# Value sums of two neighbouring key tiles issued together in the three cross attentions of a four-layer decoder

## The chip, the cores and the metric

The kernel runs on one core of a Trainium2 chip. The core has TensorE (matmul, PE in the profile), VectorE (DVE), ScalarE (ACT), GpSimd (POOL) and SyncE (SP, which starts most DMAs). Each engine works through its own stream of instructions in order, and they wait for each other through semaphores. The metric is the device time of one execution in microseconds; lower is better.

## What is computed

A decoder of four layers on a batch of 4 sequences of 256 tokens, width 128. Each layer adds a self attention, a cross attention over 512 context tokens and a feed-forward part to the residual stream. The change is in the cross attentions of layers 0, 1 and 2. Layer 2's stands for all three; layer 0 adds a mask, layer 1 projections of queries, keys and values.

```
q, k, v = split(query), split(key), split(value)        # 16 heads of 8
scores = einsum('bhqd,bhkd->bhqk', q, k) / sqrt(8)
attn = softmax(scores, axis=-1)                         # over 512 keys
ctx = einsum('bhqk,bhkd->bhqd', attn, v)                # the value sums
x = x + merge(ctx) @ w_concat.T
```

Layer 3's cross attention has no softmax and is not touched.

## The kernel before

The three cross attentions are called X0, X1 and X2. Each does 4 batches x 16 heads. The unit of work is a step: two heads with a part of the queries or keys, 64 steps in each attention. The program of every engine is written by hand as a loop over slots, `cross_slot(use, t, ...)`, and every engine issues its share of slot `t` at the same place in the order. `LEAD` is 20: in slot `t` TensorE makes the scores of step `t` (for the row maxima) and the exponents' arguments of step `t - 20`. So slots 0 to 19 have scores alone, 20 to 63 both, 64 to 83 exponents alone, and slots 24 to 87 have sums.

In a slot TensorE does, in this order:

- `pair_step` (L632): the scores of two heads (L629) into one bank of a ring of two, `ps_s0` and `ps_s1`, and the exponents' arguments of two heads (L608) into the banks `ps_e0` and `ps_e1`, four of these in a slot, each bank filled in two halves. They alternate: e0, scores, e0, e1, scores, e1. In X0 a mask is put into each exponent bank first by a matmul with the identity (L606). A bank e0 or e1 is filled again only when ScalarE has taken the exponent of what was in it (`exped`), and a score bank only when VectorE has taken the maxima of it (`maxed`).
- after a batch's last scores, the turn of the maxima (L568).
- the value sums `sums(use, g, k, ...)` (L672), from 24 on: `g` is a group of four heads and `k` one of four key tiles of 128 keys. The four matmuls of one call (one for each head, f32, 32 columns each, side by side in the array) are shown by the profile as eight. All four `k` of a group add up in `ps_v`; after the last, ScalarE copies it (L1384, `lifted`) and only then may the next group start.
- the turn of the group copied last (L577, `turn_group`), every fourth slot, which takes a bank of the score ring too; VectorE normalises from it (L1895, L1903).
- at the end of a batch its close (L585), output projection (L593) and the turn for the next stage (L554).

ScalarE in a slot: the lift of a group where one is due, then the exponents of e0 and e1 (L1396). It writes them to a ring of seven buffers `pts`, and waits with `pt_free` until the sums of the step that lay there before are done. VectorE: the maxima of a score bank (L1860 in X0, L1864 in X1 and X2), and the rest.

The call with `k` needs the exponents of all four heads. The function `sums` waits for `exped` of the step `last_step`, here `4 * g + 2 + k // 2`: the same step for k=0 and k=1, and the next for k=2 and k=3. In slot `t` the call is that of `divmod(t - 24, 4)`.

X0's slots run behind the first self attention, with the start of the expert layer behind them. X1's first 20 are woven into the second self attention (`l1_attention`), its last behind the start of the next expert layer (`swiglu_tail`). X2's slots stand beside `l2_slot` and `chain`, the work on other batches of the layers before and behind.

Of the kernel before, what the change touches and what calls it, by code (L numbers as in the profile page):

```python
# [124 lines left out]
def close_slot(use, b):  # L125
    return 21 + 8 * b if use == A0 else 40 + 16 * b
# [116 lines left out]
def build(nc, d, out, ctx):  # L243
# [3 lines left out]
    def semaphore(name):  # L247
        return ctx.enter_context(nc.semaphore(name))
# [71 lines left out]
    def rows_by_head(tile):  # L320
# [66 lines left out]
    score_ps, maxed, exp_ps, exped, summed, lifted, turned, weighed = (  # L387
        semaphore(n) for n in ("score_ps", "maxed", "exp_ps", "exped", "summed", "lifted", "turned", "weighed"))
# [147 lines left out]
    def tensor_program():  # L536
# [3 lines left out]
        def claim(name):  # L540
            if name in free:
                pe.wait_ge(*free.pop(name))
# [21 lines left out]
        def turn_max(use, b, tile):  # L564
            n = BATCH0[use] + b + 1
            i = tile()
            pe.wait_ge(max_split, n)
            pe.transpose(ps_s[i][0:96, 0, 0:64].bitcast(BF16), mparts[:].rearrange("p a s c -> p (a s c)"),  # L568
                         ident_b[:]).then_inc(max_ps, 1)
            free[f"s{i}"] = (max_T, n)  # L570

        def turn_group(use, g, tile):
            n = GROUP0[use] + g + 1
            i = tile()
            pe.wait_ge(lifted, n)
            for q in range(TPB):
                m = pe.transpose(ps_s[i][:, 0, q * P:(q + 1) * P], outT[:, g % 2, q * P:(q + 1) * P], ident)  # L577
            m.then_inc(turned, 1)
            free[f"s{i}"] = (weighed, n)

        def turn_close(use, b):
            claim("m")
            pe.wait_ge(*closed_at(use, b))
            for i, t in enumerate(tiles(b)):
                m = pe.transpose(ps_m[:, i * P:(i + 1) * P], xn[:, t, :], ident)  # L585
            m.then_inc(close_ps, 1)
            free["m"] = (close_T, CLOSE_AT[use, b])

        def project_out(use, b, w, tile):
            i = tile()  # L590
            pe.wait_ge(close_T, CLOSE_AT[use, b])
            for j, t in enumerate(tiles(b)):
                m = pe.matmul(ps_s[i][:, 0, j * P:(j + 1) * P], qT[:, t * P:(t + 1) * P], w, start=True, stop=True)  # L593
            m.then_inc(out_ps, 1)
            free[f"s{i}"] = (x_done, X_AT[use, b])
# [68 lines left out]
        def sums(use, g, k, last_step, nkt, values):  # L664
            if k == 0:
                claim("v")
            pe.wait_ge(exped, 2 * (STEP0[use] + last_step) + 2)
            b = g // 4
            for j in range(GROUP):
                step = 2 * g + j // 2 if use == A0 else 4 * g + 2 * (j // 2) + k // 2  # L670
                pt = pts[use][step % len(pts[use])]
                m = pe.matmul(ps_v[j * COLS:(j + 1) * COLS, 0:S], values(b * nkt + k, g % 4 * GROUP + j),  # L672
                              pt[:, j % 2, k % 2, :], start=(k == 0), stop=(k == nkt - 1),
                              tile_position=(0, j * COLS))
            return m
# [125 lines left out]
        def cross_slot(use, t, w_out, following, tile=ring):  # L801
            if t == 0 and use != X0:
                pe.wait_ge(d_ones, 192)
                pe.wait_ge(d_cfill, CFILL[use])
            if t == LEAD[use] and use == X0:
                pe.wait_ge(farT_done, B)
            if t == LEAD[use] + 4:
                pe.wait_ge(d_vload, 16 * {X0: 1, X1: 2, X2: 3}[use])
            if t < STEPS[use] + LEAD[use]:
                pair_step(use, t, tile)  # L810
            if t % 16 == 1 and t > 1 and t < 80:
                turn_max(use, (t - 17) // 16, tile)
            g, k = divmod(t - LEAD[use] - 4, 4)
            if 0 <= g < 16:
                m = sums(use, g, k, 4 * g + 2 + k // 2, 4, cross_values)
                m.then_inc(summed, 1)
                free["v"] = (lifted, GROUP0[use] + g + 1)
            g, rest = divmod(t - LEAD[use] - 8, 4)
            if rest == 0 and 0 <= g < 16:
                turn_group(use, g, tile)  # L820
            for b in range(B):
                at = t - close_slot(use, b)
                if at == 2:
                    turn_close(use, b)
                if at == 3:
                    project_out(use, b, w_out, tile)
                if at == 6 and following:
                    turn_norm(following, b)
# [2292 lines left out]
```

## Time and profile before

| | us |
|---|---|
| median of 3 runs | 1241.89 |
| lowest, highest | 1233.96, 1242.09 |
| span of the profiled execution | 1242.7 |
| TensorE busy in it | 1039.3 (84%) |
| VectorE busy | 795.0 (64%) |
| ScalarE busy | 611.8 (49%) |
| chain that ended last: TensorE, VectorE, ScalarE | 62%, 27%, 5% |
| value sums of X0 to X2 (L672), matmuls busy | 132.4, 1536 of them |

The profiled execution is one run of the program under the hardware profiler; every duration below is from it, and its span is to be set beside the times of the runs without it.
### The profile page before, as it was taken

How to read it: one execution, taken by the hardware profiler on the slowest of the kernel's cores; microseconds unless marked ns; L12 is line 12 of the kernel's file. 1: busy time of each engine (PE TensorE's matmuls, PEld its weight loads, DVE VectorE, ACT ScalarE, POOL GpSimd, SP SyncE). 2: the span in 40 equal slices, each digit the busy share in tenths (PEclk: the TensorE clock that was granted, in tenths of full speed). 3: DMA queues.
4: the chain of work that ended last, by engine and by line, in shares of the span. 5: the costliest groups of instructions: out<-in, count | busy, mean ns of one | idle time of the engine just before them, and what ended most of it. 6: DMA issues, size and time to landing. Idle time of an engine off the chain costs nothing.

```text
span 1242.7 us, 19890 instructions
## 1 busy us (share of the span) xinstructions
PE 1039.3 (84%) x7649; PEld 556.7 (45%) x7649; DVE 795.0 (64%) x1984; ACT 611.8 (49%) x1018; POOL 252.3 (20%) x309
## 2 busy tenths in 40 slices
PE   5777699999899975788877889999658878869999
PEld 4233223333677652355542333566323334437757
DVE  7786867731315468887767883777687886575412
ACT  2456356666334437678753777323125555333342
POOL 2933400000000225577641000001131001000000
PEclk9789879999999986566765999999867888779999
DMA  8332140000000300077014202600102100000000
GB/s 303 95 89 69 39 167 2 2 2 1 1 1 1 102 35 1 1 216 143 1 45 141 101 2 36 109 1 3 49 26 72 59 1 2 34 1 1 1 9 9
DMA packets 34786, 61.25 MB, mean 49 GB/s; under 512 B 4771, under 2 KB 25076, under 8 KB 33092
## 3 DMA queue, kind: packets, MB, share of 16 engines
q1 hardware_dynamic: 33828, 58.64, 16.5%
q8 instruction: 62, 1.02, 0.3%
q10 hardware_dynamic: 864, 1.33, 0.3%
q14 instruction: 32, 0.26, 0.1%
HBM read 42.91 MB, written 16.65 MB: 48 GB/s over the span
## 4 chain that ended last, share of the span: by engine, by line
PE 62%; DVE 27%; ACT 5%; issue 4%; DMA 1%; POOL 1%; SPq 0%; DVEq 0%; ACTq 0%; POOLq 0%
PE ps_s L879 10%; PE ps_e L869 9%; PE ps_v L672 7%; DVE mx L1864 5%; PE ps_e L608 5%; PE ps_s L629 3%; PE ps_e L606 3%; PE ps_e L973 2%; DVE ps_s L1860 2%; DVE mx L1854 2%; PE ps_s L960 2%; ACT work L1396 2%; PE ps_s L1124 1%; PE ps_v L1144 1%; DVE work L2339 1%
## 5 line engine op out<-in xcount | busy, mean ns | idle before, releaser
L1396 ACT ACTIVATE work<-ps_e 128x512 f32<-128x512 f32 x448 | 250.7, 598 | 144.3 <-PE ps_e L608 139.1
L2618 POOL TENSOR_TENSOR rstd<-rstd,halves 128x2 f32<-128x2 f32 x52 | 36.6, 705 | 699.5 <-DVE rstd L1807 699.4
L1864 DVE TENSOR_REDUCE mx<-ps_s 128x2 f32<-128x1024 f32 x128 | 154.0, 1222 | 30.0 <-PE ps_s L629 28.5
L629 PE MATMUL ps_s<-ctx_stack,q_stack 49*128 49x512 bf16 (+1 forms) x384 | 129.0, 452 | 46.0 <-DVE mx L1864 33.7
L1498 ACT ACTIVATE work<-ps_s,keep 128x512 f32<-128x512 f32 x136 | 93.0, 687 | 140.3 <-PE ps_s L879 137.3
L608 PE MATMUL ps_e<-q_stack,ctx_stack 52*128 52x256 bf16 (+1 forms) x768 | 151.4, 298 | 9.1 <-ACT work L1396 3.6
L672 PE MATMUL ps_v<-work,vaug 128*32 128x256 f32 x1536 | 132.4, 421 | 4.6 <-ACT work L1384 4.6
L869 PEld LDWEIGHTS ps_e<-ffn_w,work 128*128 128x128 f32 x960 | 118.9, 197 | 21.6 <-issue 20.5
L879 PE MATMUL ps_s<-xnT,ffn_w 128*128 128x512 f32 x240 | 118.4, 617 | 3.6 <-ACT work L1498 3.6
L869 PE MATMUL ps_e<-ffn_w,work 128*128 128x128 f32 x960 | 120.7, 281 | 0.8 <-DVE x L2050 0.8
L2060 DVE SCALAR_TENSOR_TENSOR x<-ps_e,gates,x 128x128 f32<-128x128 f32 x128 | 38.9, 346 | 123.4 <-PE ps_e L869 120.3
L1860 DVE CUSTOM_DVE_ANT_0 ps_s<-ps_s,work 128x512 f32<-128x512 f32 x128 | 86.0, 717 | 29.1 <-PE ps_s L629 29.1
L608 PEld LDWEIGHTS ps_e<-q_stack,ctx_stack 52*128 52x128 bf16 (+1 forms) x768 | 45.0, 97 | 105.2 <-ACT work L1396 49.5
L629 PEld LDWEIGHTS ps_s<-ctx_stack,q_stack 49*128 49x128 bf16 (+1 forms) x384 | 29.6, 97 | 72.2 <-DVE mx L1864 46.7
L879 PEld LDWEIGHTS ps_s<-xnT,ffn_w 128*128 128x128 f32 x240 | 41.7, 195 | 41.9 <-issue 25.3
L672 PEld LDWEIGHTS ps_v<-work,vaug 128*32 128x32 f32 x1536 | 31.7, 112 | 49.8 <-issue 36.7
L606 PE MATMUL ps_e<-work,ident_b 128*128 128x512 bf16 x128 | 51.8, 404 | 2.3 <-issue 2.3
L2677 POOL TENSOR_TENSOR work<-work 128x1536 f32<-128x1536 f32 x14 | 47.9, 3441 | 0.9 <-ACT work L1642 0.8
L1376 ACT ACTIVATE xnT<-ps_m 128x256 f32<-128x256 f32 x36 | 13.7, 382 | 61.9 <-PE ps_m L554 60.1
L1854 DVE TENSOR_REDUCE mx<-ps_s 128x4 f32<-128x1024 f32 x32 | 38.1, 1220 | 9.4 <-PE ps_s L624 9.1
L1895 DVE RECIPROCAL rsum<-ps_s 128x8 f32<-128x8 f32 x48 | 9.7, 203 | 48.9 <-PE ps_s L577 48.7
L577 PE MATMUL ps_s<-keep,work 128*128 128x128 f32 x128 | 29.3, 312 | 12.9 <-ACT work L1384 6.5
(379 smaller groups left out, 1821.5 us busy)
## 6 DMA issues: line engine op xcount, KB each, us to landing
q_stack<-q_scr SPq DMA_DIRECT2D x32, 192.0 KB
ffn_w<-in_L0f_w SPq DMA_DIRECT2D x1, 4608.0 KB, 15.9
ffn_w<-in_L1f_w SPq DMA_DIRECT2D x1, 3456.0 KB, 12.9
q_scr<-parts SPq DMA_DIRECT2D x16, 192.0 KB, 2.1
c_scr<-ffn_w SPq DMA_DIRECT2D x12, 256.0 KB, 7.1
kx_scr<-ffn_w SPq DMA_DIRECT2D x12, 256.0 KB, 4.1
ctx_stack<-kx_scr SPq DMA_DIRECT2D x2, 1536.0 KB
ctx_stack<-c_scr SPq DMA_DIRECT2D x2, 1536.0 KB
```

What stands on the lines that cost most here:

```text
L606: pe.matmul(bank[name], ident_b[:], far_k[:, b, k:k + 2, :].rearrange("p k q -> p (k q)"), start=True, stop=False, skip_group_check=True)
L608: m = pe.matmul(bank[name][:, half * S:(half + 1) * S], stack[p0:p0 + n_rows, pair, k * P:(k + 1) * P], q_stack[p0:p0 + n_rows, b, pair, : ...
L629: return pe.matmul(ps_s[i][:, parity, :], q_stack[p0:p0 + n_rows, b, pair, part * P:(part + 1) * P], ctx_stack[p0:p0 + n_rows, pair, b * S ...
L672: m = pe.matmul(ps_v[j * COLS:(j + 1) * COLS, 0:S], values(b * nkt + k, g % 4 * GROUP + j), pt[:, j % 2, k % 2, :], start=(k == 0), stop=( ...
L869: m = pe.matmul(bank[name][:, i * P:(i + 1) * P], hid[:, j, (t0 + i) * P:(t0 + i + 1) * P], w2(e, j), start=(j == 0), stop=(j == FJ - 1))
L879: pe.matmul(bank[name], w1_of(st, e, j), xnT[:, g * 512:(g + 1) * 512], start=True, stop=True).then_inc(UPS[st], 1)
L1396: act.activation(pt[:, parity, :, :].rearrange("p k q -> p (k q)"), bank[f"e{parity}"], ACT.Exp).then_inc(exped, 1)
L1498: act.activation(hid_unit(st, u)[:, j, :], bank[f"h{n % 2}"], ACT.Gelu_apprx_tanh, bias=b1).then_inc(HIDS[st], 1)
L1854: m = dve.tensor_reduce(mx[:, b, :, pair, :], ps_s[i][:].rearrange("p a (q k) -> p a q k", q=TPB), AX, ALU.max, negate=True)
L1860: m = dve.tensor_tensor_reduce(ps_s[i][:, parity, :], ps_s[i][:, parity, :], far_q[:, b * TPB + part, :], 1.0, -3e38, ALU.add, ALU.max, mx ...
L1864: m = dve.tensor_reduce(mx[:, b, :, pair, part], ps_s[i][:], AX, ALU.max, negate=True)
L2677: pool.tensor_tensor(c, c, l1_s[:, HALVES[n], :], ALU.add).then_inc(added, 1)
```

## The change

The call of `sums` was made once in each of 64 slots. Now it is made in every second slot, where `k` is 0 or 2, for `k` and `k + 1` one after the other. The argument `last_step` is written as before with the even `k`; for `k + 1` it has the same value. The increments of `summed` are as many as before, and in the same order. ScalarE's, VectorE's, GpSimd's and SyncE's streams are the same, instruction for instruction.

```diff
--- before.py
+++ after.py
@@ -811,9 +811,9 @@
             if t % 16 == 1 and t > 1 and t < 80:
                 turn_max(use, (t - 17) // 16, tile)
             g, k = divmod(t - LEAD[use] - 4, 4)
-            if 0 <= g < 16:
-                m = sums(use, g, k, 4 * g + 2 + k // 2, 4, cross_values)
-                m.then_inc(summed, 1)
+            if 0 <= g < 16 and k % 2 == 0:
+                sums(use, g, k, 4 * g + 2 + k // 2, 4, cross_values).then_inc(summed, 1)
+                sums(use, g, k + 1, 4 * g + 2 + k // 2, 4, cross_values).then_inc(summed, 1)
                 free["v"] = (lifted, GROUP0[use] + g + 1)
             g, rest = divmod(t - LEAD[use] - 8, 4)
             if rest == 0 and 0 <= g < 16:
```

Two places in TensorE's stream. The first is in X0, where scores are made: from the second half of the exponents of slot k=0 (`ps_e1`) over the sums (`ps_v`) and the group's turn (L577) to the first score matmul of the next slot. Before:

```order
L608 MATMUL ps_e1<-q_stack,ctx_stack 128x256
L629 MATMUL ps_s1<-ctx_stack,q_stack 128x512
L608 MATMUL ps_e1<-q_stack,ctx_stack 128x256
L672 MATMUL ps_v<-work,vaug 32x256 x4
L577 MATMUL ps_s0<-keep,work 128x128 x2
L606 MATMUL ps_e0<-work,ident_b 128x512
L608 MATMUL ps_e0<-q_stack,ctx_stack 128x256
L629 MATMUL ps_s1<-ctx_stack,q_stack 128x512
```

And with the change:

```order
L608 MATMUL ps_e1<-q_stack,ctx_stack 128x256
L629 MATMUL ps_s1<-ctx_stack,q_stack 128x512
L608 MATMUL ps_e1<-q_stack,ctx_stack 128x256
L672 MATMUL ps_v<-work,vaug 32x256 x8
L577 MATMUL ps_s0<-keep,work 128x128 x2
L606 MATMUL ps_e0<-work,ident_b 128x512
L608 MATMUL ps_e0<-q_stack,ctx_stack 128x256
L629 MATMUL ps_s1<-ctx_stack,q_stack 128x512
```

The sums of k=1, which stood behind the next slot, now stand ahead of the turn; the score bank that the last row waits for is the one that slot k=0 filled. The second place is in X1, where only exponents are left: from one group's turn on. Before:

```order
L577 MATMUL ps_s1<-keep,work 128x128 x2
L608 MATMUL ps_e0<-q_stack,ctx_stack 128x256 x2
L608 MATMUL ps_e1<-q_stack,ctx_stack 128x256 x2
L672 MATMUL ps_v<-work,vaug 32x256 x4
L608 MATMUL ps_e0<-q_stack,ctx_stack 128x256 x2
L608 MATMUL ps_e1<-q_stack,ctx_stack 128x256 x2
L672 MATMUL ps_v<-work,vaug 32x256 x4
L554 MATMUL ps_m<-keep,xn 128x128 x2
L608 MATMUL ps_e0<-q_stack,ctx_stack 128x256 x2
L608 MATMUL ps_e1<-q_stack,ctx_stack 128x256 x2
L672 MATMUL ps_v<-work,vaug 32x256 x4
```

And with the change:

```order
L577 MATMUL ps_s1<-keep,work 128x128 x2
L608 MATMUL ps_e0<-q_stack,ctx_stack 128x256 x2
L608 MATMUL ps_e1<-q_stack,ctx_stack 128x256 x2
L608 MATMUL ps_e0<-q_stack,ctx_stack 128x256 x2
L608 MATMUL ps_e1<-q_stack,ctx_stack 128x256 x2
L672 MATMUL ps_v<-work,vaug 32x256 x8
L554 MATMUL ps_m<-keep,xn 128x128 x2
L608 MATMUL ps_e0<-q_stack,ctx_stack 128x256 x2
L608 MATMUL ps_e1<-q_stack,ctx_stack 128x256 x2
```

The exponents' matmuls of slots k=1 and k=2 (e0, e1, e0, e1) now follow each other with nothing between, and the sums of both key tiles come after; it is the same with slots k=3 and k=0 further down, where the batch's last slots have L554 or L593 between them.

## Rows read from the trace of the kernel before

**Rows 1.** The page: span, and one costly group (busy us, mean ns).
```profile
span 1242.7 us, 19890 instructions
...
PEclk9789879999999986566765999999867888779999
...
L1864 DVE TENSOR_REDUCE mx<-ps_s 128x2 f32<-128x1024 f32 x128 | 154.0, 1222 | 30.0 <-PE ps_s L629 28.5
```

**Rows 2.** Busy time by stretch (length, PE, PEld, DVE, ACT, POOL, clock, DMA).
```profile
720.00:770.00 50.00, 46.64 (x476) 17.11 (x472) 29.07 (x75) 39.67 (x81) 1.39 (x2) 1.00 0.01 2
...
960.00:1000.00 40.00, 32.34 (x256) 11.89 (x257) 34.17 (x61) 20.34 (x42) 0.70 (x1) 0.82 0.19 75
```

**Rows 3.** Timeline, TensorE, X0 (start, us, engine, line, operation, count, idle before).
```profile
200.94 0.39 PE L606 MATMUL ps_e<-work,ident_b 128*128 128x512 bf16 x1
...
202.23 0.64 PE L672 MATMUL ps_v<-work,vaug 128*32 128x256 f32 x8
202.80 0.44 PE L577 MATMUL ps_s<-keep,work 128*128 128x128 f32 x2
203.07 0.38 PE L606 MATMUL ps_e<-work,ident_b 128*128 128x512 bf16 x1
203.39 0.28 PE L608 MATMUL ps_e<-q_stack,ctx_stack 56*128 56x256 bf16 x1
203.80 0.39 PE L629 MATMUL ps_s<-ctx_stack,q_stack 49*128 49x512 bf16 x1
```

**Rows 4.** Timeline, ScalarE, the same slot of X0.
```profile
201.70 1.27 ACT L1396 ACTIVATE work<-ps_e 128x512 f32<-128x512 f32 x2 [0.24 <-PE ps_e L608]
```

**Rows 5.** Timeline, VectorE, end of that slot's maxima.
```profile
203.60 0.14 DVE L1860 DVE_READ_ACCUMULATOR2_ANT mx<- 128x1 f32 x1
```

**Rows 6.** Timeline, TensorE, X2, slots before the first sums.
```profile
924.55 0.28 PE L608 MATMUL ps_e<-q_stack,ctx_stack 52*128 52x256 bf16 x1
...
925.64 0.28 PE L608 MATMUL ps_e<-q_stack,ctx_stack 52*128 52x256 bf16 x1 [0.48 <-ACT work L1396]
```

**Rows 7.** Timeline, TensorE, end of X0, two sums in a row.
```profile
295.39 1.07 PE L672 MATMUL ps_v<-work,vaug 128*32 128x256 f32 x16
296.39 1.12 PE L879 MATMUL ps_s<-xnT,ffn_w 128*128 128x512 f32 x2
```

**Rows 8.** Timeline, TensorE, X1, slots without scores.
```profile
750.92 0.88 PE L608 MATMUL ps_e<-q_stack,ctx_stack 52*128 52x256 bf16 x4
751.73 0.64 PE L672 MATMUL ps_v<-work,vaug 128*32 128x256 f32 x8
...
753.38 0.88 PE L608 MATMUL ps_e<-q_stack,ctx_stack 52*128 52x256 bf16 x4
```

**Rows 9.** Timeline, TensorE, X1, a clean group with scores.
```profile
723.95 0.44 PE L577 MATMUL ps_s<-keep,work 128*128 128x128 f32 x2
724.32 0.28 PE L608 MATMUL ps_e<-q_stack,ctx_stack 52*128 52x256 bf16 x1
724.77 0.39 PE L629 MATMUL ps_s<-ctx_stack,q_stack 49*128 49x512 bf16 x1 [0.17 <-DVE mx L1864]
...
729.70 0.44 PE L577 MATMUL ps_s<-keep,work 128*128 128x128 f32 x2
```

**Rows 10.** Timeline, TensorE, X1, first exponents of a batch.
```profile
696.18 0.28 PE L608 MATMUL ps_e<-q_stack,ctx_stack 52*128 52x256 bf16 x1 [0.79 <-DMA q_stack<-mT]
```

**Rows 11.** Timeline, TensorE, X2, a stall and a filler.
```profile
996.68 0.60 PE L629 MATMUL ps_s<-ctx_stack,q_stack 49*128 49x512 bf16 x1 [2.53 <-DVE mx L1864]
...
1006.88 1.60 PE L1279 MATMUL ps_s<-ffn_w,work 128*128 128x128 f32 x12
```

**Rows 12.** Timeline, TensorE, X1 at half clock, without and with sums.
```profile
671.09 0.39 PE L608 MATMUL ps_e<-q_stack,ctx_stack 52*128 52x256 bf16 x1 [0.27 <-ACT work L1396]
...
672.39 0.39 PE L608 MATMUL ps_e<-q_stack,ctx_stack 52*128 52x256 bf16 x1 [0.21 <-ACT work L1396]
...
677.12 0.39 PE L608 MATMUL ps_e<-q_stack,ctx_stack 52*128 52x256 bf16 x1
...
679.11 0.39 PE L608 MATMUL ps_e<-q_stack,ctx_stack 52*128 52x256 bf16 x1
```

## The prediction

> **What bounds the kernel now.** I read the page first: one core, span 1242.7 us [rows 1]. The three cross attentions lie at about 160 to 300 us (X0), 650 to 775 us (X1) and 900 to 1080 us (X2). Then the busy time by stretches [rows 2]: in the middle of X1 TensorE is busy 46.64 of 50 us at full clock, in X2 32.34 of 40 us at a mean clock of 0.82. So X1 is close to TensorE-bound by its busy time and X2 is not. What limits a step, though, is read from the timeline, and there the three differ. I call one pass of `cross_slot` a slot, and by what follows from `k` the four slots of a head group P0 (k=0, with the turn of the finished group behind its sums), P1, P2, P3.
>
> In X0 a slot has two mask matmuls more, so TensorE is the limit: from 200.94 to 202.80 is one slot of 1.86 us, 1.29 of it the exponents' and scores' matmuls and 0.57 the sums (202.23 to 202.80) [rows 3]. ScalarE starts on the exponents 0.76 us after the slot begins and takes 1.27 us for both banks [rows 4], with slack. Only in P1 is there a stall: it begins at 203.07, its first score matmul would come 0.33 us later but comes at 203.80, 0.40 us late, because the ring of two score banks waits for VectorE, which is done with P0's scores at 203.74 [rows 3, 5].
>
> In X1 and X2 the same matmuls without the mask take only about 0.54 us, and 0.57 us of sums stand between two of them. What sets the pace there is the loop bank e0, exponent on ScalarE, bank free again. The rows that show this best are two slots of X2 before its sums have begun, with nothing between them: they begin at 924.55 and 925.64, 1.09 us apart, the second after 0.48 us of waiting for the exponent [rows 6]. So without sums between them two slots are no closer than 1.09 us, and with sums between them they are 1.11 us (0.54 + 0.57) apart. **The sums now fill a gap in which TensorE would wait anyway.** This decides the forecast.
>
> **What the change does.** No instruction is added or taken away: 3 x 16 groups x 4 sums, each 4 matmuls that the profile counts as 8. The sums of k=1 and k=3 come one slot earlier, behind those of k=0 and k=2. Their waits on `exped` name the same step as their neighbour's, so no new wait arises. The last sum of a group is there a slot earlier, but ScalarE lifts it at its old place. P1 and P3 lose their sums; P0 and P2 have two; P0's two now stand ahead of the turn.
>
> *Fewer changes of form.* Eight sum matmuls take 0.57 us until the next operation starts. Sixteen in a row take 1.00 us (295.39 to 296.39) [rows 7]. So a pair costs 1.00 us in place of 1.14: 0.14 us saved, 96 pairs, 13.4 us if TensorE were the limit everywhere. The Trainium skill ("TensorEngine Tiling", Key Properties) says that changing the tiling mode drains TensorE; the row agrees, with 0.14 us for a change and its way back, and by that rule alone the kernel would be the 13.4 us faster.
>
> *X0.* Slot pairs P1-P2 and P3-P0 now follow directly. The second one's first matmul needs bank e0, free after 0.76 us and half of 1.27 us and some hand-over, at 1.40 to 1.42 us; the slot is 1.29 us long. That is 0.11 to 0.13 us of new wait against 0.14 saved: zero. In P1 the 0.40 us stall goes, since the second sum now lies ahead of it (0.43 us, 1.00 less 0.57) and VectorE is done by then. Scores are still made in 9 such P1 slots behind a turn: 9 x 0.42 = **-3.8 us**.
>
> *X1, slots without scores* (the last five groups). Now a pair lasts from 750.92 to 753.38, 2.46 us; a slot whose bank e1 has to wait for its exponent lasts 0.81 us up to its sums (750.92 to 751.73) [rows 8]. Afterwards a pair is 1.09 to the second slot, 0.81 for it, 1.00 for the double sums: 2.90 us. That is +0.44 a pair, two pairs a group: 5 x 0.87 = 4.4. At the close of a batch four projection matmuls fall between P3 and P0 and cover the wait once: -0.4. **+4.0 us.**
>
> *X1, slots with scores* (ten groups). A clean group lasts 5.75 us from turn to turn (723.95 to 729.70), with a stall of 0.45 us in P1 (724.32 to 724.77) on VectorE's maxima [rows 9], which take 1.22 us each [rows 1]. Afterwards: 0.37 (turn) + 1.09 + 0.81 + 1.00 + 1.09 + 0.81 + 1.00 = 6.17 us: +0.42. VectorE needs 4 x 1.22 and under half a microsecond for the turn, 5.3 us, so it is no longer what is late; ScalarE's loop is. In other words both second halves cost 0.43, and P1's stall takes one of them back. Where the next batch's maxima come by DMA (a wait of 0.79 us ahead of the slot at 696.18) [rows 10], the other is taken in too; that is so twice. 10 x 0.42 - 2 x 0.4 = 3.4, and 0.2 less for the start at half clock (below). **+3.2 us.**
>
> *X2.* The same per clean group, but other work stands between its slots. The stall at 996.68, 2.53 us on VectorE, swallows a shifted sum whole, and twelve matmuls of 1.60 us at 1006.88, between P1 and P2, keep the exponent's wait covered, so that there the 0.14 is earned [rows 11]. Of the 16 groups I find five or six clean or nearly so (+0.42 each), the others at zero, a few below. Bounds: nothing at all, and 16 x 0.6 = +9.6. I take **+2 us**, near the lower end, since most of its stalls name VectorE.
>
> *Half clock.* Part of X1 and X2 runs at 1.2 GHz. There a slot is 1.99 us (677.12 to 679.11) and two slots without sums are 1.30 us apart (671.09 to 672.39) [rows 12]. A pair then takes 1.30 + 0.98 + 1.02 + at most 1.02 = 4.3 us against 3.98: +0.3 at most, less than at full clock.
>
> Sum: -3.8 + 4.0 + 3.2 + 2 = **+5.4 us**, 1248.1 on the profiled execution's 1242.7. That execution lies 0.8 us above the median of the runs shown (1241.9), so I predict **1247 us**.
>
> **Rivals.**
> *A, TensorE-bound after all (faster).* If ScalarE's loop took up the burst, 13.4 us of form changes and the 3.8 us of X0 would come off: 1225 us. For it speaks the busy share in X1 [rows 2]. Against it speak the two slots 1.09 us apart: TensorE waits in them with nothing else to do [rows 6]. It would decide if two bare slots took less than 1.46 us together (2.46 - 1.00), where the rows make it 1.90. A tenth of the chance; a smaller form of it, X0 gaining and X2 gaining from its covered pairs, ends within 1%.
> *B, all absorbed (same).* The loss in X1 is swallowed by VectorE and DMA waits as in X2, the gain in X0 stays: 1238 to 1242. For it: the stalls in [rows 9 to 11]. Against it: the five groups without scores have no such stall to give [rows 8].
> *C, the clock (slower).* TensorE idles about 0.5 us in each pair of X1 where it idled little. In X2 the clock, down to 0.82 in the mean, goes with TensorE's idle stretches [rows 2, 11]. If X1 fell to half clock for half its 32 pairs, each of these would take 4.3 in place of 2.9 us: 16 x 1.4 = 22 us, 1269 in all. A third of that is 1255. Against it: the bare slots at 924.55 are half idle and still run at full clock. The Trainium skill ("TensorE: Matmul & The Clock Gate", Part 1) has it that the throttled state is the default and that activity releases it; no run here shows yet how the new rhythm is judged.
>
> **How the numbers follow.** Forecast mechanism as sized (1243 to 1253) 0.58; B 0.17; C, or a loss in X2 near its upper bound, 0.16; A 0.09. One per cent, 12.4 us, is about what a measurement of this kernel can tell from no change. Above 1254.3 lie C but for its mildest cases and the tail of the forecast: 0.19. Below 1229.5 lies A: 0.08. The range 1237 to 1259 takes in B and the first third of C, and leaves out A and the rest of C, under 2 in 10.
>
> **What the profile afterwards would show.** In X0 no score matmul waits 0.4 us behind the turn, and the slot pairs last 3.7 us. In X1 slots without scores come in pairs of 2.9 us, with TensorE's idle time named after the exponents. ScalarE's idle time falls between double sums, about 0.7 us at a time. The groups with scores last 6.2 us and VectorE's stall in P1 is gone. X1 from its first sum to its last is 7 us longer, X0 4 us shorter. Wrong I would be if X1's pairs took less than 2.6 us (A), if the groups with scores kept 5.75 us (B), or if the granted clock in X1 fell below 1 (C).

## The result, and the profile after

| | before | after |
|---|---|---|
| median, lowest, highest (us) | 1241.99 (1233.96 to 1246.52) | 1265.7 (1263.25 to 1269.77) |
| ratio | | 1.0195, 95% interval 1.0156 to 1.0233 |
| span of the profiled execution | 1242.7 | 1265.0 |
| mean granted clock in it | 0.863 | 0.850 |

The kernel became 23.7 us slower. I had said 1247 us and a range up to 1259, so the forecast was wrong in size and right in sign. The page of after, to be set beside [rows 1]:

```profile
span 1265.0 us, 19890 instructions
...
PEclk9778879999999985567676997999756889779999
...
L1864 DVE TENSOR_REDUCE mx<-ps_s 128x2 f32<-128x1024 f32 x128 | 154.4, 1222 | 33.6 <-PE ps_s L629 30.5
```

The maxima take 1222 ns as before. In the clock line the 25th place (about 760 to 790 us, in X1) fell from 9 to 7, and the 29th to 31st, around X2's start, from 8, 6, 7 to 7, 5, 6. The busy time by stretches, for [rows 2]:

```profile
720.00:770.00 50.00, 40.31 (x392) 16.55 (x388) 31.83 (x74) 32.17 (x66) 0.70 (x1) 0.90 0.01 2
960.00:1000.00 40.00, 32.74 (x276) 13.14 (x276) 29.56 (x56) 21.71 (x44) 3.53 (x6) 0.79 0.28 100
```

In the middle of X1 TensorE is busy 40.31 us of 50 instead of 46.64, ScalarE 32.17 instead of 39.67, and the clock is 0.90 where it was 1.00.

A clean group of X1 with scores, TensorE's timeline (start, us, engine, line, operation, count, idle before), for [rows 9]:

```profile
730.88 0.44 PE L577 MATMUL ps_s<-keep,work 128*128 128x128 f32 x2
731.25 0.28 PE L608 MATMUL ps_e<-q_stack,ctx_stack 52*128 52x256 bf16 x1
...
732.35 0.28 PE L608 MATMUL ps_e<-q_stack,ctx_stack 52*128 52x256 bf16 x1 [0.48 <-ACT work L1396]
...
733.16 1.07 PE L672 MATMUL ps_v<-work,vaug 128*32 128x256 f32 x16
...
737.06 0.44 PE L577 MATMUL ps_s<-keep,work 128*128 128x128 f32 x2
```

From turn to turn it takes 6.18 us (730.88 to 737.06); the forecast was 6.17. Two slots without sums are 1.10 us apart with 0.48 us of waiting for the exponent, and the double sums take 1.01 us (733.16 to the next slot at 734.17). ScalarE's idle time lies between double sums, as its timeline of the same group shows:

```profile
731.70 2.20 ACT L1396 ACTIVATE work<-ps_e 128x512 f32<-128x512 f32 x4 [0.84 <-PE ps_e L608]
734.60 1.08 ACT L1396 ACTIVATE work<-ps_e 128x512 f32<-128x512 f32 x2 [0.70 <-PE ps_e L608]
```

The part of X1 without scores, for [rows 8]: one pair at half clock, one at full clock.

```profile
763.22 0.61 PE L608 MATMUL ps_e<-q_stack,ctx_stack 52*128 52x256 bf16 x4
764.51 1.09 PE L608 MATMUL ps_e<-q_stack,ctx_stack 52*128 52x256 bf16 x4 [0.68 <-ACT work L1396]
765.53 1.93 PE L672 MATMUL ps_v<-work,vaug 128*32 128x256 f32 x16
767.39 0.69 PE L577 MATMUL ps_s<-keep,work 128*128 128x128 f32 x2
...
774.74 0.40 PE L608 MATMUL ps_e<-q_stack,ctx_stack 52*128 52x256 bf16 x4
775.82 0.88 PE L608 MATMUL ps_e<-q_stack,ctx_stack 52*128 52x256 bf16 x4 [0.68 <-ACT work L1396]
776.63 1.07 PE L672 MATMUL ps_v<-work,vaug 128*32 128x256 f32 x16
777.63 0.44 PE L554 MATMUL ps_m<-keep,xn 128*128 128x128 f32 x2
```

At full clock a pair lasts 2.89 us (774.74 to 777.63; forecast 2.90, before 2.46). At half clock it lasts 4.17 us (763.22 to 767.39). So the groups of X1 are what I worked out; but part of them runs at half clock, where in the trace of before all of this part ran at full clock.

**The measure used below.** A run's granted clock is a mean over two levels, 1.2 and 2.4 GHz, so the time at half clock is 2 x (1 - clock) x span. From the two pairs, a microsecond at half clock costs (4.17 - 2.89) / 4.17 = 0.31 us. With that the difference of two kernels is split in two: what the clock accounts for, and the rest. The split is an estimate: it takes the price of one place for the whole program. The runs bear it out roughly: among the runs of before, the span grows with the time at half clock by 0.26, 0.29 and 0.30 us per us in three series and by 0.18 in the fourth. At 0.27 the clock's shares below would be an eighth smaller.

### The profile page after: what moved, and what is told of

The parts are those of the page before. It is cut to its first block, busy times and chain, and to the rows that moved or that the text cites. A ratio compares the mean times of both kernels' runs of the same rounds, so it can differ in the third digit from the quotient of the medians.

```text
span 1265.0 us, 19890 instructions
## 1 busy us (share of the span) xinstructions
PE 1041.4 (82%) x7649; PEld 571.3 (45%) x7649; DVE 795.8 (63%) x1984; ACT 608.8 (48%) x1018; POOL 252.1 (20%) x309
## 4 chain that ended last, share of the span: by engine, by line
PE 62%; DVE 25%; ACT 6%; issue 4%; DMA 1%; POOL 1%; SPq 0%; DVEq 0%; ACTq 0%; POOLq 0%
PE ps_s L879 10%; PE ps_e L869 9%; PE ps_v L672 8%; PE ps_e L608 5%; DVE mx L1864 5%; ACT work L1396 3%; PE ps_s L629 3%; PE ps_e L606 3%; PE ps_e L973 2%; PE ps_s L960 2%; DVE mx L1854 2%; DVE ps_s L1860 1%; PE ps_s L577 1%; PE ps_s L1124 1%; PE ps_v L1144 1%
## 5 line engine op out<-in xcount | busy, mean ns | idle before, releaser
L1396 ACT ACTIVATE work<-ps_e 128x512 f32<-128x512 f32 x448 | 251.2, 599 | 161.1 <-PE ps_e L608 155.5
L1864 DVE TENSOR_REDUCE mx<-ps_s 128x2 f32<-128x1024 f32 x128 | 154.4, 1222 | 33.6 <-PE ps_s L629 30.5
L672 PE MATMUL ps_v<-work,vaug 128*32 128x256 f32 x1536 | 117.7, 430 | 5.6 <-ACT work L1384 5.6
L672 PEld LDWEIGHTS ps_v<-work,vaug 128*32 128x32 f32 x1536 | 43.3, 118 | 50.9 <-issue 21.9
L577 PE MATMUL ps_s<-keep,work 128*128 128x128 f32 x128 | 30.9, 327 | 12.1 <-ACT work L1384 6.6
```

What stands on the lines that cost most here:

```text
L1396: act.activation(pt[:, parity, :, :].rearrange("p k q -> p (k q)"), bank[f"e{parity}"], ACT.Exp).then_inc(exped, 1)
L1864: m = dve.tensor_reduce(mx[:, b, :, pair, part], ps_s[i][:], AX, ALU.max, negate=True)
```

## The experiments

Line numbers behind line 815 are shifted by a few lines in some of these kernels, so the sums' exponents are L1396 in one and L1400 or L1405 in another.

### The change as a whole, and each attention alone

The whole change again, and X0, X1 and X2 changed alone, each with this condition (X1's is shown):

```diff
             g, k = divmod(t - LEAD[use] - 4, 4)
+            if 0 <= g < 16 and use in (X1,):
+                if k % 2 == 0:
+                    for kk in (k, k + 1):
+                        sums(use, g, kk, 4 * g + 2 + k // 2, 4, cross_values).then_inc(summed, 1)
+                    free["v"] = (lifted, GROUP0[use] + g + 1)
-            if 0 <= g < 16:
+            elif 0 <= g < 16:
                 m = sums(use, g, k, 4 * g + 2 + k // 2, 4, cross_values)
```

> The changed kernel once more, for a second trace and more times. Theory L (the exponent loop: the sums covered ScalarE's exponent, and where nothing covers it TensorE waits): the groups of X1 without scores last 6.2 us, those with scores 6.2, whatever the clock does elsewhere; X1 from its first sums to its last is 7 us longer than before at full clock. Theory K (the clock: most of the 23 us come from stretches at half clock that the idle gaps bring about): the half clock stretches lie again in X1's last third and in X2, and the time follows their number. If the 4.6 us that the first profile was behind before any changed slot is chance, they are not there this time.

> Only X0 issues its sums in pairs. My prediction's step: 9 stalls of 0.4 us go, the pairs cost nothing: -3.8 us. The profile of the changed kernel showed X0 level instead (VectorE's last slots of X0 as late as its first). Theory L: between -4 and +1 us. Theory K: the same, with any loss in a half clock stretch inside X0.

> Only X1 issues its sums in pairs. Theory L: +7 us, of it 4 in the five groups without scores and 3 in the ten with scores, 6.2 us a group; up to +9 with the end of X1. Theory K: +12 or more, of it 4 or more in a half clock stretch in the part without scores, as in the first profile of the change. No effect of X1: within 2 us.

> Only X2 issues its sums in pairs. Theory L: +2 us, since VectorE's stalls and other work cover it (bounds 0 to +10). Theory K: +5 to +10 with more half clock stretches in X2 and behind it, where the layers after X2 were 3 us later in the first profile of the change. The parts should add up to the whole within 3 us under L; under K they need not.

Measured beside 23 runs of before with a median of 1241.83 us. The span column is the difference of the mean spans; "half clock" is the mean time at half clock over all runs of the kernel, less that of before (333 us) in the same series; "rest" is the span column less 0.31 times the half clock. All but the ratio are in us.

| kernel | median, ratio (interval) | span | half clock | x 0.31 | rest |
|---|---|---|---|---|---|
| whole change | 1264.1, 1.0167 (1.0129 to 1.0204) | +21.5 | +35 | 10.8 | 10.7 |
| X0 alone | 1242.95, 1.0008 (0.9983 to 1.0033) | +1.0 | +4 | 1.4 | -0.4 |
| X1 alone | 1256.1, 1.0098 (1.006 to 1.0136) | +13.6 | +15 | 4.8 | 8.7 |
| X2 alone | 1248.39, 1.0038 (1.0016 to 1.006) | +5.5 | +8 | 2.5 | 3.0 |

The medians add up: 1.1 + 14.3 + 6.6 = 22.0 us, beside 22.3 for the whole. X0 gives nothing, X1 costs twice its forecast and X2 three times. About half of the loss goes with the clock. The standard error of the mean time at half clock is 2 to 6 us for each kernel, so each split is good to 1 to 2 us only.

The 4.6 us that the first profile of the change lay behind ahead of any changed slot were chance: X0's first sums stand at 168.83 us in before, 173.43 in after, 168.67 in the whole change again, and at 172.36 in x1_tail below, which leaves X0 alone.

**X0.** Where the gain of 3.8 us went is seen in single groups of X0. TensorE's timeline of before, the group in which the turn of the maxima (L568) stands in P1:

```profile
185.36 0.44 PE L577 MATMUL ps_s<-keep,work 128*128 128x128 f32 x2
...
188.07 0.64 PE L672 MATMUL ps_v<-work,vaug 128*32 128x256 f32 x8
...
189.45 0.39 PE L629 MATMUL ps_s<-ctx_stack,q_stack 49*128 49x512 bf16 x1 [0.21 <-DVE mx L1860]
...
190.41 0.64 PE L672 MATMUL ps_v<-work,vaug 128*32 128x256 f32 x8
```

And with X0 alone changed:

```profile
179.08 0.44 PE L577 MATMUL ps_s<-keep,work 128*128 128x128 f32 x2
...
186.79 0.44 PE L577 MATMUL ps_s<-keep,work 128*128 128x128 f32 x2
...
190.87 0.39 PE L629 MATMUL ps_s<-ctx_stack,q_stack 49*128 49x512 bf16 x1 [0.85 <-DVE mx L1865]
...
191.83 1.07 PE L672 MATMUL ps_v<-work,vaug 128*32 128x256 f32 x16
...
196.60 0.44 PE L577 MATMUL ps_s<-keep,work 128*128 128x128 f32 x2
...
211.42 0.39 PE L629 MATMUL ps_s<-ctx_stack,q_stack 49*128 49x512 bf16 x1 [0.43 <-DVE mx L1865]
```

The group ahead (179.08 to 186.79) takes 7.71 us instead of 8.10: its stall is gone, as forecast. In the group with L568, P2's score matmul comes 4.08 us after the turn, before it was 4.09: VectorE, which has to take the turned maxima out of the score bank, sets that moment. The sums of P1 used to run inside this wait; now the wait is 0.85 us instead of 0.21, and the double sums stand behind it. The group takes 9.81 us instead of 9.33. P1's own stall stays as well in this group (0.69 us before, 0.68 now). So the gain of 0.39 in one group is given back in the next.

From turn to turn the nine groups with scores behind a turn (g = 1 to 9) come in three kinds. The five odd ones gain 0.38 to 0.40 each, 2.0 us together. The two that close a batch (g = 4 and 8) gain nothing, 9.06 and 9.07 us for 9.04: P1's stall is gone, but behind the output projection (L593), which takes a score bank too, stands a new one of 0.43 us, at 211.42. Of those with L568, g = 2 loses 0.48, and g = 6 takes 11.30 us for 9.34. The busy time of that last group, before and with X0 alone changed:

```profile
220.26:229.60 9.34, 8.44 (x71) 2.73 (x68) 6.55 (x21) 5.14 (x10) 0.00 (x0) 1.00 0.02 4
```

```profile
221.40:232.70 11.30, 9.62 (x72) 3.15 (x68) 6.97 (x23) 5.00 (x9) 0.00 (x0) 0.85 0.02 4
```

Its clock is 0.85, and its double sums take 1.87 us (226.79 to 228.66) instead of 1.00: about 3 us at half clock, some 1.5 us of time. Each of the four traces with all of X0 in pairs (after, the whole change again, this one, fill below) has one group of 11.30 to 11.32 us among its two with L568 inside X0's scores (g = 2, 6), the other being 9.81 or 9.82; the two traces of before have 9.33 and 9.34 us there. So even in X0, which I had held to be the safe gain, the clock has a share.

### Only the end of X1 (x1_tail)

```diff
-            if 0 <= g < 16 and use in (X1,):
+            if 0 <= g < 16 and use == X1 and g >= 10:
```

> Pairs only in the last six groups of X1, which have no scores beside them (24 slots). By the forecast's terms +4.0 us and nothing else. If X1's further loss of some 6 us is the clock and arises where TensorE idles at each pair without any scores to fill, it is here: +10 us, with a stretch at half clock in the trace. If it arises in the groups with scores, +4 us and full clock.

Measured 1250.45 us, ratio 1.0067 (1.0035 to 1.0098); mean span +7.8 us. This part can be cut out exactly in every trace: from the router's matmul (L836, `ps_m<-keep,xnT 128x8`) to the first matmul of the next feed-forward part (L960, 128x512). The busy time by stretches between these two, for before, this kernel, X1 alone, and the whole change again:

```profile
745.96:773.09 27.13, 25.29 (x267) 9.51 (x263) 8.38 (x42) 21.67 (x44) 0.69 (x1) 1.00 0.15 25
```

```profile
744.87:782.10 37.23, 30.58 (x258) 11.57 (x254) 8.38 (x42) 21.64 (x43) 0.70 (x1) 0.72 0.11 18
```

```profile
747.97:785.21 37.24, 30.58 (x258) 11.60 (x254) 8.38 (x42) 21.64 (x43) 0.69 (x1) 0.73 0.10 16
```

```profile
751.59:788.11 36.52, 29.77 (x259) 11.44 (x255) 8.39 (x42) 21.63 (x43) 0.70 (x1) 0.77 0.20 29
```

The columns are length, busy time of TensorE (and of its weight loads), VectorE, ScalarE and GpSimd, granted clock, DMA share and GB/s. The first trace of after has 35.33 us at 0.81. Take off 0.31 us for each us at half clock (20.8, 20.1, 16.8 and 13.4 us): 30.8, 31.0, 31.3 and 31.2 us are left, against 27.13. **That is +3.7 to +4.2 us, and the forecast's term for this part was +4.0.** The other 4 to 6 us are the clock. Half-clock time of 13 to 21 us stands in this part in all four traces, where the first trace of before had none. Over the 12 runs of x1_tail the picture is weaker: their time at half clock is 5 us above that of before, with a standard error of 7 (single runs lie between 293 and 377 us), which makes 1.5 us by the clock and 6.3 rest. So the 20.8 us in its trace are not what each of its executions shows.

### Before, once more (same)

> The kernel before once more, for a second trace of it: which of its stretches at half clock lie at the same place again, and how far the lengths of X0, X1 and X2 agree between two executions of one program. If the stretches at half clock are set by the program, X1 has none in its last 50 us here too; if chance has a part in them, it may have one of 3 to 10 us, as the kernel with X0 alone changed had.

Its span was 1242.9 us, and in the same stretch:

```profile
743.56:773.55 29.99, 28.65 (x267) 9.97 (x263) 8.38 (x42) 21.84 (x44) 0.70 (x1) 0.83 0.12 22
```

So chance has a part: the same program lost 2.9 us there to 10.2 us at half clock (0.28 us each). With X0 alone changed the stretch is 29.95 us at 0.83, with X2 alone 28.16 at 0.94; the three kernels warm, x0_some and both further down, which leave this part alone, have 27.14 us at 1.00 each. So seven traces without the pairs have 1.00 (four of them), 0.94, 0.83 and 0.83, and the four with them 0.72, 0.73, 0.77 and 0.81. The two groups do not overlap, but the change makes more of something that was there already.

### Filling the gaps (fill)

The changed kernel with sum matmuls that nobody reads, in the slots with k=1 of X1 and X2, where TensorE waits for ScalarE:

```diff
+            if 0 <= g < 16 and k == 1 and use != X0 and t < STEPS[use] + LEAD[use]:
+                for j in range(GROUP):
+                    pe.matmul(ps_v[j * COLS:(j + 1) * COLS, S:2 * S], vaug_pad[:, 0:COLS], keep[:, 0:S],
+                              start=False, stop=True, tile_position=(0, j * COLS), skip_group_check=True)
```

> The changed kernel with four more sum matmuls (0.57 us at full clock) in each slot with k=1 of X1 and X2, where TensorE now waits for ScalarE; they write the second half of ps_v, which nobody reads, 32 times in all. Theory L (ScalarE sets the pace: two slots without sums are 1.09 us apart, and 0.54 + 0.57 fits in it): they cost at most 1 us where the clock stays, so about 1264 us again, and the slot pairs of X1 keep 2.9 us. Theory K (part of the loss is the clock, which falls because TensorE idles in the gaps): X1 stays at full clock and the time falls towards 1256 us. Rival, TensorE is the bound: 32 x 0.57 = 18 us more, 1282 us.

Measured 1258.41 us, ratio 1.0148 (1.0113 to 1.0183). 32 times 0.57 us = 18 us of matmuls were added, and the kernel took 5.7 us less than without them by the medians, and 4.5 by the mean spans, with a standard error of 1.9. The same stretch of X1:

```profile
749.65:786.12 36.47, 32.09 (x290) 11.92 (x286) 8.39 (x42) 21.48 (x43) 0.70 (x1) 0.77 0.20 30
```

It is as long, and at the same clock, as in the whole change again (36.52 us at 0.77), with 2.3 us more of TensorE's time in it. The rival "TensorE is the bound" (1282 us) falls: what is put into the gaps is free. Over the six runs the time at half clock was 11 us above that of before, not 35: 3.5 us by the clock, 13.5 rest. Theory K gets its direction, but not in full: X1's end did not return to full clock.

### The pair in the other slots (late)

```diff
             if 0 <= g < 16:
-                m = sums(use, g, k, 4 * g + 2 + k // 2, 4, cross_values)
-                m.then_inc(summed, 1)
-                free["v"] = (lifted, GROUP0[use] + g + 1)
+                if k % 2:
+                    for kk in (k - 1, k):
+                        sums(use, g, kk, 4 * g + 2 + k // 2, 4, cross_values).then_inc(summed, 1)
+                    free["v"] = (lifted, GROUP0[use] + g + 1)
```

> The pairs in the other slots: P1 has the sums of k=0 and k=1, P3 those of k=2 and k=3, in all three attentions. The turn of the finished group now stands alone between P0 and P1. Theory L: in X1 and X2 the turn (0.37 us) lies in a gap in which TensorE waits for ScalarE, so a clean group of X1 takes 5.80 us instead of 6.17 (before: 5.75), and a group costs about 0.4 us less than in the changed kernel: 16 in X1 and the clean ones of X2, some 8 to 9 us. In X0 nothing is gained, since VectorE's maxima hold up P1 just as before and the longer sums come behind them: 9 x 0.43 = 3.9 us more than before. Sum about 1264 - 9 + 3 = 1258 us. If the loss had nothing to do with the place of the pair but only with its length, 1264 us again. Theory K adds: X1 at full clock again, 1252.

Measured 1249.2 us, ratio 1.0075 (1.0043 to 1.0106), 15 us less than the change with as many pairs of the same length. TensorE's timeline in the part of X1 without scores:

```profile
756.64 1.07 PE L672 MATMUL ps_v<-work,vaug 128*32 128x256 f32 x16
757.64 0.40 PE L608 MATMUL ps_e<-q_stack,ctx_stack 52*128 52x256 bf16 x4
758.72 0.88 PE L608 MATMUL ps_e<-q_stack,ctx_stack 52*128 52x256 bf16 x4 [0.68 <-ACT work L1397]
759.53 1.07 PE L672 MATMUL ps_v<-work,vaug 128*32 128x256 f32 x16
760.53 0.40 PE L608 MATMUL ps_e<-q_stack,ctx_stack 52*128 52x256 bf16 x4
761.20 0.41 PE L577 MATMUL ps_s<-keep,work 128*128 128x128 f32 x2 [0.27 <-ACT work L1385]
761.61 0.87 PE L608 MATMUL ps_e<-q_stack,ctx_stack 52*128 52x256 bf16 x4
762.42 1.07 PE L672 MATMUL ps_v<-work,vaug 128*32 128x256 f32 x16
```

A group lasts 5.78 us (756.64 to 762.42; expected 5.80): the turn at 761.20 now lies in the gap between two slots without sums. The stretch to the feed-forward part takes 29.18 us, wholly at full clock:

```profile
752.19:781.37 29.18, 24.66 (x272) 10.53 (x271) 8.38 (x42) 22.89 (x45) 0.70 (x1) 1.00 0.17 28
```

2.05 us more than before, with half of the gaps covered. The expected 1258 us without the clock, 1252 with it, were still too high; the runs spent 328 us at half clock, 6 less than before. The rest, +11.0 us, hardly differs from that of the change (10.7), because X1 gains what X0 loses: from first turn to last, X0 takes 125.44 us in late and 122.66 in after (before: 123.03), and X1, with 0.31 us taken off for each us at half clock, 96.3 against 98.5. By this measure the clock makes nearly all of the difference between the two kernels.

### A sum inside the slot (mid)

One sum a slot, as before, but in X1 and X2 those of k = 1, 2 and 3 between the matmuls for bank e0 and those for e1 (the place in `pair_step` only; `cross_slot` passes the sum in as `between`):

```diff
             if exps:
                 exps_of(use, h, 0, 1)
+                if between:
+                    between()
                 exps_of(use, h, 1, 0)
```

> The other way round: one sum a slot as before, but in X1 and X2 the sums of k=1, 2 and 3 stand inside their slot, between the second half of bank e0 and the first of e1, so that ScalarE has an exponent to take while they run. Theory L: ScalarE's gaps behind the sums (0.3 us a slot pair in the part of X1 without scores) close; a pair there goes from 2.46 to 2.24 us, 2 us in all, and where VectorE is late nothing changes: 1232 to 1240 us. Rival: VectorE's maxima and the order of the banks bound it, 1242 us. If the scores behind the sums now come too late for VectorE, it is slower: 1250.

Measured 1278.4 us, ratio 1.0271 (1.0219 to 1.0323): slower than everything else here, where I expected a gain. Two rows of ScalarE's timeline in X1 at full clock give the part of it that is order:

```profile
731.87 2.28 ACT L1405 ACTIVATE work<-ps_e 128x512 f32<-128x512 f32 x4 [0.32 <-PE ps_e L608]
734.46 0.60 ACT L1405 ACTIVATE work<-ps_e 128x512 f32<-128x512 f32 x1 [0.32 <-PE ps_e L608]
```

The exponent of e0 takes 0.60 us, and in that time TensorE does 0.57 us of sums and only then 0.27 us for e1, so ScalarE runs dry. A group takes 6.31 us (turns at 729.70 and 736.01). More than half of the loss is the clock: 405 us at half clock, 71 more than before, 22 of 37 us by the price above; without its two longest runs (1285.76 and 1288.31 us) it is 56 more, 17 of 33 us. In X1's end:

```profile
765.00:780.00 15.00, 15.00 (x91) 4.43 (x92) 2.70 (x12) 8.04 (x16) 0.70 (x1) 0.50 0.00 1
780.00:795.00 15.00, 13.36 (x84) 3.53 (x88) 0.86 (x4) 8.48 (x16) 0.00 (x0) 0.50 0.22 37
```

TensorE is busy 15.00 of 15.00 us by its records and has half its clock, and it keeps that clock through the next 15 us, 13.36 of them busy. So "TensorE idles, and therefore the clock falls" is too simple. The Trainium skill ("TensorE: Matmul & The Clock Gate", Part 1) says that throttling is the default and activity releases it; this row does not agree, as far as activity is what the records call busy.

### A version that beats both

Two small edits of the kernel before. First, the unread sums in the four slots of X1 and of X2 that have no sums yet, [rows 6]:

```diff
+            if use != X0 and LEAD[use] <= t < LEAD[use] + 4:
+                for j in range(GROUP):
+                    pe.matmul(ps_v[j * COLS:(j + 1) * COLS, S:2 * S], keep[:, 0:COLS], keep[:, 0:S],
+                              start=False, stop=True, tile_position=(0, j * COLS), skip_group_check=True)
```

> The kernel before, with four more sum matmuls into the unread half of ps_v in each of the four slots of X1 and of X2 that have no sums yet (t = 20 to 23), where TensorE waits 0.48 us for ScalarE: eight times 0.57 us. Theory L (a gap filled with work costs nothing): 1242 us. Theory K (the clock falls where TensorE waits, and rises again where it does not): the stretch at half clock at X1's start, which reaches about 20 us beyond the start of these slots in the kernel before, ends earlier, and the time falls by up to 0.3 us for each us less at half clock, 1236 to 1240 us. Rival, TensorE-bound: 8 x 0.57 = 4.6 us more, 1246 us.

Second, in X0 the pair k=0, k=1 in those groups alone where nothing gives the gain back:

```diff
             if 0 <= g < 16:
-                m = sums(use, g, k, 4 * g + 2 + k // 2, 4, cross_values)
-                m.then_inc(summed, 1)
+                early = use == X0 and g < 10 and g % 2 == 1
+                for kk in ((0, 1) if k == 0 else () if k == 1 else (k,)) if early else (k,):
+                    sums(use, g, kk, 4 * g + 2 + k // 2, 4, cross_values).then_inc(summed, 1)
```

> X0 alone is changed, and only k=0 and k=1 of the groups g = 1, 3, 5, 7 and 9 are issued together: those in which no turn of maxima (L568) follows in P1. X1 and X2 as before. Theory from the trace of x0_only: these groups lose the stall of P1 and take 7.71 us instead of 8.11 from turn to turn, 5 x 0.4 = 2 us off, and the groups with a turn of maxima keep their 9.33 us: 1240 us. Rival, the stall only moves to P3, where the next group's sums now stand as before: 1242 us.

And both together:

> The kernel before with the two small changes that each came out a little below it: four unread sum matmuls in each of the slots t = 20 to 23 of X1 and X2, and in X0 k=0 and k=1 issued together in the groups g = 1, 3, 5, 7 and 9. If both gains are real they add up: 2 us from X0's stalls and 2 to 6 us from less time at half clock in X2, 1233 to 1237 us. If warm's was chance: 1239 us.

Measured beside before's 1240.66 us (23 runs; the first two) and 1240.69 us (17 runs; both):

| kernel | median | ratio (interval) | span | half clock |
|---|---|---|---|---|
| fillers in slots 20 to 23 (warm) | 1239.04 | 0.9976 (0.9952 to 1.0) | -2.9 | -16 |
| X0's clean groups paired (x0_some) | 1238.27 | 0.9995 (0.9966 to 1.0023) | -1.0 | 0 |
| both | 1232.94 | 0.9951 (0.9926 to 0.9975) | -6.8 | -21 |

The two together are the one kernel here whose interval lies clearly below 1: 0.5% under before. The mean spans have standard errors of 1.3 to 1.6 us, so that 6.8 is more than 2.9 and 1.0 together proves nothing; nearly all of the 6.8 us goes with the clock (21 us at 0.31). Its profiled execution is the shortest with the highest clock, from the view of spans and clocks:

```profile
core 0: 1225.8 us, clock 0.884
```

Of warm, TensorE's timeline at the start of X2, beside [rows 6]:

```profile
924.99 0.28 PE L608 MATMUL ps_e<-q_stack,ctx_stack 52*128 52x256 bf16 x1
...
925.53 0.64 PE L816 MATMUL ps_v<-keep 128*32 128x256 f32 x8
926.10 0.28 PE L608 MATMUL ps_e<-q_stack,ctx_stack 52*128 52x256 bf16 x1
```

The slots are 1.11 us apart with the filler and were 1.09 apart without it: the gap takes it in. The busy time of the stretch behind it, first before, then warm:

```profile
924.00:960.00 36.00, 29.61 (x231) 10.47 (x229) 28.29 (x43) 19.57 (x39) 7.16 (x7) 0.76 0.13 39
```

```profile
924.00:960.00 36.00, 29.70 (x288) 10.94 (x286) 31.62 (x47) 22.69 (x45) 7.17 (x7) 0.95 0.20 61
```

The clock is 0.95 instead of 0.76. With both edits it is 0.95 too, and in the second trace of before 0.76 again. Three further traces without fillers in which X2's first sums come within 3 us of warm's (x0_some, x2_only, x0_only) have 0.76, 0.78 and 0.79. Over 150 us from X2's first value sum on, the clock is 0.82 and 0.83 in the two traces of before and 0.83 to 0.86 in eight of the other kernels without fillers (mid: 0.75), 0.89 in warm, and 0.91 in both and in fill. The other engines get further in the same 36 us. At X1's start, where I had expected it, nothing moved. In the trace of x0_some a pair of groups takes 17.03 us instead of 17.43:

```profile
178.99 0.44 PE L577 MATMUL ps_s<-keep,work 128*128 128x128 f32 x2
...
186.26 0.44 PE L577 MATMUL ps_s<-keep,work 128*128 128x128 f32 x2
...
196.02 0.44 PE L577 MATMUL ps_s<-keep,work 128*128 128x128 f32 x2
```

I had expected 7.71 and 9.33; it is 7.27 and 9.76, since the turn in the odd groups itself stands 0.43 us later, behind two sums. The sum is the expected one: 0.40 us for each of five groups, 2 us. X0 from its first sum to its last turn shows it: 129.43 us in x0_some and in both, 131.46 and 131.47 in the two traces of before. The comparison of whole times alone can't tell it from nothing.

## Why the prediction was wrong

**What held.** The reading of what paces X1: two slots without sums stay 1.08 to 1.10 us apart, the double sums take 1.0 us, pairs last 2.89 us and groups 6.18 us, where I had 2.90 and 6.17. VectorE's stall in P1 is gone there. X1's end costs 3.7 to 4.2 us at equal clock, where I had 4.0. Rival A is excluded: 18 us of further matmuls cost nothing, and rival B too: the groups did not keep 5.75 us. One thing in my words was too narrow: I named the loop of bank e0. At 1.08 to 1.10 us for two banks (the rows at 734.60 and 731.70 in after's ScalarE timeline) ScalarE itself takes as long as the loop, so with nothing between the slots it is simply full. For the sum it makes no difference.

**The step that failed first: the clock.** The sum put the clock's change at nothing and left it to rival C, which had a chance of 0.16 (with a large loss in X2) and whose price was X1's alone (22 us if half its pairs fell, 1255 for a third of that). The runs have 35 to 44 us more at half clock in the whole program: 11 to 14 us. C's sign came: the granted clock in X1 fell below 1; but it did so in the second trace of before too (0.83 in X1's end), so that sign alone could not tell the change from chance. In the traces X1's end, with 13 to 21 us at half clock, gives 4 to 6 us, and X0 some 1.5. Behind X2's last turn, where no instruction is changed, five of the traces with pairs in X1 or X2 (after, the whole change again, X1 alone, X2 alone, fill) take 164.0 to 164.1 us at a clock of 0.91, and four others (the two of before, X0 alone, x1_tail) 160.9 at 0.93: 3 us more, which the forecast had nowhere. The remaining five (late, mid, warm, x0_some and both) take 159.4 to 162.4 us. The remaining part can't be placed: from X2's first value sum on, 150 us have a clock of 0.83 in after and 0.85 in the whole change again, no less than before's 0.82 and 0.83, and other places differ between executions of one program. C was right in kind, and a case with both, the rhythm as sized and some clock, should have been the likeliest. My reason against it was that the bare slots at 924.55 are half idle and still at full clock. They are the start of a stretch that falls to half clock a few microseconds later, and with the four slots filled of which these are two, its clock was 0.95 instead of 0.76. I read that row as evidence against the rival; with what comes behind it, it was rather evidence for it.

**X0, the term of -3.8 us.** It measured -0.4 (the rest of X0 alone), and from X0's first sum to its last turn nothing is gained: 131.5 to 131.8 us in the four traces with its pairs, 131.5 in the two of before. The 0.4 us are earned in the five odd groups, as I had said. I counted every P1 slot behind a turn as alike, 9 of them; at a batch's close the stall comes back behind the projection (L593), and where the turn of the maxima follows, VectorE's work lies one slot further on, the sum that used to fill that wait is gone, and 0.48 us are lost, with 1.5 more where the clock falls. I had listed L568 and L593 among TensorE's work but not asked what else takes a bank of the score ring.

**X1 and X2, at equal clock.** +8.7 us for X1 alone against 7.2, within what the split can tell. X2 +3.0 against 2, inside its bounds of 0 to 9.6. The traces say the same with less noise. With 0.31 us taken off for each us at half clock, X1 from its first turn to its last takes 91.5 us in both traces of before and 98.0 to 98.9 in four with its pairs, 6.5 to 7.4 us more. X2 from its first sum to its last turn takes 135.3 to 137.0 us in six traces without its pairs and without fillers, and 137.6 to 138.9 in three with them: about 2 us.

Together at equal clock, by the runs: -0.4 + 8.7 + 3.0 = 11.3 us, and 10.7 for the whole, where my sum was 5.4. So of the 22 us about half is the rhythm, of which half was forecast, and about half is the clock.

**What stays open.** Why the clock falls more often, and so the cause of about half of the loss. It is shown that the traces with the change's pairs in X1's end run it at 0.72 to 0.81, and those with its sums as before at 0.83 to 1.00, and that fillers lower the time at half clock (the changed kernel from 35 to 11 us above before, the kernel before by 16, with standard errors of 4 to 5). It is not shown that idle time is what decides: late leaves TensorE about as idle (24.66 of 29.18 us busy) and stayed at 1.00 there, and mid has 15 us at 0.50 in which its records leave no gap. One execution a trace, and chance of 10 us at half clock in one place, are too little for more.

## What to carry to other kernels

Gathering small pieces of an engine that has slack saves changes of form and takes cover away from the engine that paces the loop; ask what filled the gaps before. On TensorE a gap has a second price, the clock: set the granted clock of the stretch beside its length, and compare kernels over many runs by time at half clock, since single traces of one program differ by 10 us at half clock in one place. Where a gap can't be closed, matmuls that nobody reads are cheap to try: here they cost 0.02 us a slot, and the 36 us from the last two of X2's on ran at 0.95 instead of 0.76.

## What the hardware showed that I had not expected

- TensorE busy 15.00 of 15.00 us at a granted clock of 0.50 (mid, 765 to 780 us).
- 18 us of added matmuls made a kernel no slower, and by the medians 5.7 us faster (1258.41 against 1264.1 us). With 0.57 us of them in each of the four slots ahead of X2's first sums, the 36 us from 924 us on ran at 0.95 instead of 0.76 to 0.79.
- Two executions of one program: X1's end in 27.13 us at clock 1.00 and in 29.99 us at 0.83, with spans of 1242.7 and 1242.9 us.
